# Down weights of the experts loaded behind all gate and up weights, and the first four page loads issued from ScalarE's queue

## What is computed

```python
def ffn(x):                                   # x: 2048 tokens x 128, after a layer norm
    shared = (silu(x @ sh_gate) * (x @ sh_up)) @ sh_down
    logits = x @ gate_w                       # 32 experts, inner width 256
    e = argmax(logits); xs = x * sigmoid(max(logits))
    # each token goes through its own expert's weights
    routed = (silu(xs @ r_gate[e]) * (xs @ r_up[e])) @ r_down[e]
    return shared + routed

x = x + 0.5 * ffn(layernorm(x))
x = x + attention(layernorm(x))               # 16 heads of 8, low-rank projections
x = x + 0.5 * ffn(layernorm(x))
```

## Time and profile before

| what | us |
|---|---|
| median of three runs (lowest, highest) | 635.89 (635.8, 636.3) |
| the profiled execution, its own time | 637.31 |
| its span, first to last instruction | 635.6 |
| mean granted clock of TensorE | 0.927 of full speed |
| PE busy over the span | 551.2 (87%) |
| DVE busy | 466.8 (73%) |
| ACT busy | 381.8 (60%) |

### The profile page before, as it was taken

One profiled execution on the slowest core, in us unless ns is written; L12 is line 12 of the kernel. 1 busy time (PEld: TensorE's weight loads), 2 busy tenths in 40 slices (PEclk: granted clock), 3 DMA queues, 4 the chain that ended last, 5 costly groups with the idle time before them and its releaser, 6 DMA issues.

```text
span 635.6 us, 13810 instructions
## 1 busy us (share of the span) xinstructions
PE 551.2 (87%) x4594; PEld 217.9 (34%) x4594; DVE 466.8 (73%) x871; ACT 381.8 (60%) x815; POOL 149.3 (23%) x238
## 2 busy tenths in 40 slices
PE   2875999955588999999999999999999985799991
PEld 2642444433231222222222222222224444534440
DVE  6771444446579899999999999999996584534442
ACT  2310344313513899999999999999997742134440
POOL 2176344515410000000000000000000043214552
PEclk9995999987755999999999999999999997989996
DMA  8994222122341000101001010000000000111114
GB/s 271 350 362 150 77 83 86 53 76 90 102 156 50 2 3 1 52 2 37 19 2 52 2 52 3 2 2 2 3 2 2 3 26 27 31 40 54 50 41 142
DMA packets 39280, 40.70 MB, mean 64 GB/s; under 512 B 5193, under 2 KB 33502, under 8 KB 39216
## 3 DMA queue, kind: packets, MB, share of 16 engines
q1 hardware_dynamic: 36144, 35.58, 17.8%
q0 software_dynamic: 3072, 4.28, 2.0%
HBM read 26.85 MB, written 14.88 MB: 66 GB/s over the span
## 4 chain that ended last, share of the span: by engine, by line
PE 69%; DVE 10%; DMA 6%; issue 5%; POOL 3%; ACT 3%; another core or an unknown queue 1%; SPq 1%; POOLq 0%; ACTq 0%; DVEq 0%
PE bank L1472 22%; PE pair L1449 18%; PE pair L1333 7%; PE bank L1350 5%; DVE rowmax L1088 4%; DMA xe<-rows 4%; PE pair L1342 3%; POOL rows L536 2%; PE bank L1244 2%; ACT oT L777 2%; PE bank L1461 1%; PE bank L1482 1%; PE bank L1321 1%; PE bank L1401 1%; PE pair L1172 1%
## 5 line engine op out<-in xcount | busy, mean ns | idle before, releaser
L1088 DVE TENSOR_REDUCE rowmax<-pair 128x1 f32<-128x1024 f32 x256 | 294.5, 1218 | 14.3 <-PE pair L1449 14.3
L764 ACT ACTIVATE arena<-bank 128x512 f32<-128x512 f32 x500 | 271.1, 597 | 30.2 <-PE bank L1461 23.1
L1449 PE MATMUL pair<-k_stack,q_stack 48*128 48x512 bf16 x512 | 163.0, 404 | 10.8 <-DVE rowmax L1088 9.8
L1472 PE MATMUL bank<-arena 128*32 128x256 f32 x2048 | 160.9, 392 | 3.0 <-ACT oT L777 0.7
L1461 PE MATMUL bank<-q_stack,k_stack 51*128 51x512 bf16 x500 | 152.1, 386 | 0.4 <-ACT arena L764 0.4
L1034 DVE TENSOR_TENSOR arena<-pair,arena 128x256 f32<-128x256 f32 x64 | 39.6, 619 | 74.4 <-ACT arena L671 60.9
L545 POOL DMA_INDIRECT y<-yb,slot_token x64 | 62.9, 983 | 87.1 <-ACT yb L676 65.0
L1472 PEld LDWEIGHTS bank<-arena 128*32 128x32 f32 x2048 | 43.4, 108 | 98.5 <-issue 63.5
L1333 PE MATMUL pair<-w_exp,xeT 128*64 x128 | 69.0, 622 | 0.4 <-ACT xeT L666 0.4
L1335 PE MATMUL pair<-w_exp,xeT 128*64 128x512 f32 x128 | 68.9, 621 | 0.0
L1449 PEld LDWEIGHTS pair<-k_stack,q_stack 48*128 48x128 bf16 x512 | 28.4, 95 | 117.4 <-DVE rowmax L1088 84.1
(11 more groups left out here) (196 smaller groups left out, 601.1 us busy)
## 6 DMA issues: line engine op xcount, KB each, us to landing
xe<-rows SPq DMA_DIRECT2D x64, 66.0 KB
w_exp<-in_r_gate SPq DMA_DIRECT2D x4, 1024.0 KB
w_exp<-in_r_up SPq DMA_DIRECT2D x4, 1024.0 KB
w_exp<-in_r_down SPq DMA_DIRECT2D x4, 1024.0 KB
rows<-q_stack SPq DMA_DIRECT2D x1, 2112.0 KB, 8.6
rows<-empty_row SPq DMA_DIRECT2D x32, 66.0 KB
q_stack<-y SPq DMA_DIRECT2D x8, 256.0 KB, 3.4
q_parts<-arena SPq DMA_DIRECT2D x12, 128.0 KB, 2.1
```

Of the source, the lines that this page charges most:

```text
L764: nc.scalar.activation(prob[c % 2 * GH + head_of(u, c, k)], ring_bank("score", STEPS * u + i), ACT.Exp, scale=SCALE).then_inc(prob_ready, 1)
L1088: nc.vector.tensor_reduce(rowmax[u % 2][:, m:m + 1], pair[j % 2][:, :], AX_X, ALU.max).then_inc(smax_read, 1)
L1449: ins = nc.tensor.matmul(pair[j % 2][:, part * BANK:(part + 1) * BANK], q_stack[r][rows, half, l, t * P:(t + 1) * P], k_stack[r][rows, l, ...
L1472: ins = nc.tensor.matmul(bank[6][32 * h:32 * (h + 1), cols], v_grp[u % 2][:, c, h, :], prob[c % 2 * GH + h][:, cols], start=(c == 0 and w ...
```

## The change

- SP issues the four gate and four up transfers first and the four down transfers behind them. The downs count on a semaphore of their own, `downs_loaded`.
- PE's wait at the start of the turns asks for 8 transfers in place of 12, and PE waits for the four downs ahead of the first `down` of `ffn(0)`.
- In `ffn(0)`, page loads 0 to 3 are no longer issued by SP. ACT waits for `scattered` and issues them, ahead of `x_out(0)`. SP, which waits for `scattered` too, goes on with clears 0 to 3 at once and then enters its loop with load 4. `ffn(1)` is as before.

```diff
-
+            for e in range(0, EXPERTS, step):
                 sp.dma_start(w3[:, e:e + step, 2 * INNER:],
-                             r_down[e:e + step].rearrange("e (p c) h -> p e (c h)", c=2)).then_inc(experts_loaded, 16)
+                             r_down[e:e + step].rearrange("e (p c) h -> p e (c h)", c=2)).then_inc(downs_loaded, 16)
...
                 for r in range(4):
-                    load(r, r)
-                if n == 0:
-                    for r in range(4):
+                    if n:
+                        load(r, r)
+                    else:
                         clear(r)
...
+                if n == 0:
+                    act.wait_ge(scattered, 16 * TILES)
+                    for r in range(4):
+                        nc.scalar.dma_start(xe[r][:, :], rows_dram[0].rearrange("(s q) r -> s q r", s=2)[:, r * PAGE:(r + 1) * PAGE, :])\
+                            .then_inc(xe_loaded[r], 16)
                 act.wait_ge(shh_sb, 8 * n + 2 * SH_AHEAD[n])
                 x_out(0, 0)
...
                 def down(j, r, e):
+                    if n == 0 and j == 0:
+                        pe.wait_ge(downs_loaded, 16 * 4)
...
-                pe.wait_ge(experts_loaded, 16 * 12)
+                pe.wait_ge(experts_loaded, 16 * 8)
```

More of the change, by code:

```diff
@@ L272, in build @@
         experts_loaded = sem("experts_loaded")
+        downs_loaded = sem("downs_loaded")
         consts_ready = sem("consts_ready")
```

## The result

| | before | changed kernel |
|---|---|---|
| median of the runs taken beside each other | 636.13 us (17 runs) | 637.67 us (17 runs) |
| ratio after / before, 95% interval | | 1.003, 1.0018 to 1.0042 |
| profiled execution | 637.31 us, span 635.6 | 637.67 us, span 635.9 |

The changed kernel is 0.3% slower, some 1.9 us, with an interval of 1.1 to 2.7 us. One of its 17 runs took 1316.14 us and is left out of the ratio; the other 16 took 635.9 to 640.26. The ratios here are worked out from all the runs that count and not from the two medians, whose own ratio can differ by some 0.1% (here 1.0024). So it is not the case that was thought likeliest.

What follows compares the result with a forecast made beforehand. The prediction took the scatter's landing, page issue and page 1's data to bound the kernel. Costs of 0.5 + 0.4 = 0.9 us, less 0.45 and 0.2, left 0.25: 635.89 + 0.25, about 636.2 us, range 634.5 to 638.2.

Steps and rivals of the forecast that it cites:

- the case that was thought likeliest: Whole kernel: time within 0.2% (1.3 us) of no change, 634.6 to 637.2 us; chance 0.69.
- What bounds the kernel there: Before the first layer's routed turns: last scatter's landing, page issue, 5.14 us of page data, transpose 1 at 59.71 us.
- Part 1: Weight transfers, gate and up first: saving 0, cost 0 to 0.05 us, taken as 0; first `down` has its weights.
- Part 2: Page loads 0 to 3 issued by ACT, each 0.56 to 1.06 us: cost and saving on the path 0.
- Part 3: Clears 0 to 3 at 53.8 us beside pages 0 and 1: page 1 later by 0 to 0.9 us, taken 0.5.
- Part 4: Load 4 issued at about 59 us, sharing page 2's two engines: 0 to 0.9 us, taken 0.4.
- Where the delay goes: After `gate_up(1)`: of 0.9 us later, the clock's return gives back 0.45, later page waits take 0.2, leaving 0.25 us.
- Rival A: First page loads: ACT's own queue brings page 1 with page 0, 1.1 us gained plus 0.3, 634.5 us; chance 0.12.
- Rival B: First turns: clears and load 4 go ahead of pages 1 to 3, clock returns later, +2.5, 638.4 us; chance 0.20.
- The number: Whole kernel's median: about 636.2 us predicted, with a range of 634.5 to 638.2 us.
- the forecast's own range: Whole kernel, from the ends of the forecast's costs and a gain of some 0.4 us: 635.4 to 637.0 us.

Runs made afterwards that it cites:

- the third experiment: Against the kernel before: page loads 0 to 3 issued by ACT, clears 0 to 3 behind SP's loop, weights in the old order; 635.96 us, ratio 0.9994.

## Why the prediction was right and wrong

- **What bounds the kernel there:** right. The chain is again the scatter's landing, page issue, page data, transpose 1. Every kernel that made page 1 later by 0.6 us or more came out slower by 0.24 to 0.3%.
- **Part 1, order of the weights, 0:** right; 1.0004 for it alone. The first `down` had its weights.
- **Part 2, issue on ACT, 0 on the path:** right, though the bounds were too narrow: ACT's first issue took 1.16 us, beyond the 1.06, and four of them 5.46 us. The slack that was named, up to the first copy of a transposed page, covered it. With the clears away the ACT part measures 0.9994.
- **Part 3, clears beside pages 0 and 1, taken 0.5, bounds 0 to 0.9:** this is the step that failed. It measured 7.28 − 5.80 = 1.5 us, above its upper bound. The cost was worked out as the clears' share of the engines' time alone, 0.9 us if it fell nowhere idle, and as far as the packets tell that share was paid in full. What it put at nothing is the slower start of the page data, some 0.6 us: packets of 60 ns or more that sum to 2.3 to 2.7 us in place of 0.6 to 1.4. Clears and page 0 did not arrive together either, but at 0.86 and 1.45 us after the issue. I had counted on the sparse beginning of the page data (share 0.03) to take the clears for free; that is where they did harm.
- **Part 4, early load 4, taken 0.4:** wrong, it is 0. Load 4 was issued at 58.87 in the third experiment, and page 2 was still there in time. Part 3 was 1.0 us too low and part 4 0.4 too high, so that together, 0.9, they were only some 0.6 short. That is luck, not a good reading.
- **Where the delay goes, 0.9 to 0.25:** wrong, and this moved the forecast to no difference at all. I let the clock come back at the same moment and the later waits take up some. Neither gave anything back. The waits for pages behind 65 us were 3.8 us and not less than 3.0. The clock came back at 66.0 in place of 64.9, but not because it follows the delay: in the kernel with the page loads on ACT alone, with the same delay at transpose 1, it was back at 64.6. Over all traces it rose from 3.6 to 6.7 us behind transpose 1. From the first page issue to transpose 31 the five kernels without clears beside the pages took 67.0 us on average, and the three with four took 68.6. So of 1.4 us at transpose 1 all was there at transpose 31, 1.6 us, and the time shows 1.9, interval 1.1 to 2.7. Why nothing was given back, even with the early clock, is open.
- **Rival A, faster:** its condition was tested and fell. Pages from ACT's queue alone (experiment 3) come no sooner than from SP's, 5.80 and 5.94 us, and keep the share of 0.14. Where both kernels' rows agree so, that bears out the Trainium skill, "DMA: Bandwidth & Descriptors", section "Issuing engines are not separate DMA queues", by which another issuing engine saves issue time only. The split of the first four loads then brought page 1 in right behind page 0 in another way, without a measurable gain.
- **Rival B, slower:** nearest to what happened, 638.4 against a median of 637.67. The clears did go against the pages and the clock did come back later. But load 4 had no part in it that shows, and the clock came back 1 us later and not 3. The Trainium skill's page "DMA: Bandwidth & Descriptors", section "Queues, rings and completion order", has each engine serve its queues in turn. The trace agrees where clears and pages are on the page engines together: page packets keep their 28 ns, and there are fewer of them. But turns alone give the 0.9 us of my bound and not 1.5, and nothing at all for a clear that has gone before the first page packet, which still cost 0.6.
- **The number:** that 637.67 lies in the range owes something to luck. The range was stretched to 638.2 to take in rival B; the sum said 636.2, and the forecast's own range ended at 637.0.

The lesson of the number: with a cost of 1.5 at transpose 1, nothing for load 4 and nothing given back, the same sum gives 635.89 + 1.5 = 637.4, close to the median of 637.67.

## What to carry to other kernels

Moving the first loads to a second queue is not free just because the loads themselves are unhurt: look at what moves up on the first queue. Transfers that no one is waiting for, put beside the reads that everyone is waiting for, cost more than their bytes; keep them behind, as the kernel before did. Don't count on a later rise of the clock to give half of a delay back: here it rose at times that the delay did not explain, and none of the delay came back. Before a mean per packet is read as slower packets, part the stretch in two; here it was a slow start and an unchanged pace. And look in the trace whether an experiment did what it was meant to: the clear meant for two engines ran on sixteen.

## What the runs showed of the hardware

- Page reads of 528-byte rows took 28 ns per packet at the median, with no clears or with up to eight issued beside them. What the clears changed was the start: page packets of 60 ns or more within the first 3.3 us summed to 0.6 to 1.4 us without clears and to 2.3 to 2.7 beside four.
- A write of 66 KB whose packets had all started 0.3 us before the first packet of the reads still made the reads' last packet start 0.5 us later (5.82 us after the first issue, against 5.25 to 5.35).
- ACT's first issue of a page load took 1.15 to 1.16 us, SP's first 0.69. The second took about 0.55 on both; the third and fourth took 1.75 and 1.94 us on ACT in the changed kernel, and 1.35 and 1.52 on SP in the kernel before.
- An issue of half a page costs SP what one of a whole page does, 0.58 us against 0.56. Halving transfers to use more engines doubled the issue time, and from transpose 1 to 31 the kernels took 8 to 11 us longer; that SP's time is the cause is not shown.
